# Two reorderings inside the eight slots of a chunked delta-rule scan: right sides ahead of the state updates on TensorE, and the matching swaps on VectorE and ScalarE

## The chip, the cores and the metric

The kernel runs on one NeuronCore of a Trainium2 chip. The metric is the device time of one execution in microseconds (us); the median over runs counts. TensorE is called PE below, with its weight loads (PEld) apart, VectorE is DVE, ScalarE is ACT, GpSimd is POOL, and SyncE (SP) issues all DMAs of the inner loop.

## The reference, cut to what matters

The input is 32 sequences of 512 tokens with 256 features: 8 heads of 32. A recurrent layer keeps for each head a 32x32 state S and takes two steps for each token: one that decays S, one that writes the pair (k, v). Both subtract what the state already answers to k:

```
bS = einsum('bhk,bhkv->bhv', b_t, S)
S  = exp(g)[..., None] * S + a_t[..., None] * bS[:, :, None, :] + k_t[..., None] * v_t[:, :, None, :]
o  = einsum('bhk,bhkv->bhv', q_t, S)
```

Here q, k, v are silu(x W), g and beta are projections too, and k is normalised. The outputs are gated, normalised for each head and projected by Wo. Then follow x + attention, a layer norm, one dense layer with a low-rank addition, and a second layer norm.

## The kernel before, in words

The work is cut into 32 groups of 512 tokens (32 sequences, 16 tokens each). Within a group the scan is solved by chunks: 16 steps of 8 tokens are made into a small triangular system, whose inverse (t_t) is worked out one group ahead, so that the scan itself is only small matmuls of 32x32 tiles, four heads side by side on the array. A group has 8 chunks, and the main loop has one **slot** for each: n = 0 to 7. PE does in a slot, in this order:

- `deltas()` (L707, 64 matmuls): inverse (t_now) times the turned right sides (x_now) of the slot before, into p2_bank.
- `updates()` (L695 and L699, 64 matmuls each, interleaved): the change of the state into ds_bank and the correction of the outputs into o_bank, from parts and delta, which ACT copied from p2_bank in the slot before.
- `right_sides()` (L716, 128 matmuls): the state s_now times keys and queries uq_now, into p1_bank.
- a piece of dense work for other groups, another for each slot: dense4 (L614), dense5 (L585: two sums for each of two inputs), dense6 (L667), dense7 (L678, transposes). Slots 0 and 1 hold besides two packages each of `scores()` (L687), which build the small system of the next group; the first of slot 0 waits for keys and queries staged by DMA (uq_a from uqv). L562 are the projections.

DVE does in a slot `update` (called by scan_part: it waits for p3_filled, the end of updates(); two halves of the outputs at L1063, then moved = state + ds_bank at L1069), `turn_right_sides` (called by turn_part: it waits for p1_filled, the end of right_sides(); subtracts the values at L1076 and transposes at L1079), and then its dense work. In slots 1 and 7 a piece of dense work stands between the two. In slot 7 that is the sum of x_row with the projected outputs (L1242), and after the turn DVE writes uqv for the next group but one (L1253, L1258), which SP then stages as uq_a (L346). In slot 5 the first dense work is L1194, which empties the banks that dense5 fills again. In slot 7 x_row's halves empty a bank that dense7 fills again.

ACT does in a slot `delta_part` (called by scan_part: waits for p3_filled and for DVE's o_added; three copies of p2_bank, L834 twice and L835) and `query_part` (waits for x_turned, DVE's transpose; one copy of the query part of p1_bank, L841), then its own dense work. POOL turns moved into the decayed state (L469).

SP has one queue, written out by hand. Its order in slot n is: t_now once deltas() is done; then, once updates() is done, aq_now (L388) and w_now (L390) for the next slot; then, once right_sides() is done and the state decayed, uq_now (L356) and s_now (L357) for the next slot:

```
sp.wait_ge(p3_filled.handle, left)
sp.dma_start(aq_now[:, :, :], ...)
sp.dma_start(by_pairs(w_now[:, :, :]), ...)
...
sp.wait_ge(state_ready.handle, kept)
sp.wait_ge(p1_filled.handle, left)
stage_first(c if n < CH - 1 else 1 - c, (n + 1) % CH)
```

The change leaves SP and POOL alone. "Block" below is the run of deltas, updates and right sides of one slot on PE.

Of the kernel before, what the change touches and what calls it, by code (L numbers as in the profile page):

```python
# [74 lines left out]
def delta_block(nc, x, xt, wq, wk, wv, wf1, wf2, wbeta, wog1, wog2, norm_w, wo, ffn_wt, ffn_b,  # L75
# [36 lines left out]
    with ExitStack() as ctx:  # L112
# [404 lines left out]
        def _(pe):  # L517
# [193 lines left out]
            def right_sides():  # L711

                for m in range(CT):
                    for b in range(GB):
                        for h in range(HPH):
                            mm = pe.matmul(p1_bank[quarter(h), m, b, :], s_now[quarter(h), m, b, :],  # L716
                                           uq_of(uq_now, m % HF)[quarter(h), m // HF, b * RQ:(b + 1) * RQ],
                                           start=True, stop=True)
                mm.then_inc(p1_filled.handle, 1)

            def slot(j, s):
# [8 lines left out]
                pe.wait_ge(set_up.handle, N_SET_UP)  # L730
                pe.wait_ge(w_in.handle, turn16)
# [93 lines left out]
        def _(act):  # L825
# [56 lines left out]
            def iteration(j, c):  # L882
# [10 lines left out]
                if there(j):  # L893
                    inverse_out(j)
                scan_part(0)
                query(0)
# [15 lines left out]

                scan_part(1)
                query(1)
# [17 lines left out]

                scan_part(2)
                query(2)
# [16 lines left out]

                scan_part(3)
                query(3)
# [24 lines left out]

                scan_part(4)
                query(4)  # L980
# [5 lines left out]

                scan_part(5)
                query(5)
# [20 lines left out]

                scan_part(6)  # L1010
                query(6)
# [5 lines left out]

                scan_part(7)
                query(7)
# [12 lines left out]
        def _(dve):  # L1032
# [91 lines left out]
            def iteration(j, c):  # L1124
# [9 lines left out]

                scan_part(0)
                turn_part(0)
# [13 lines left out]

                scan_part(1)
# [5 lines left out]
                turn_part(1)  # L1157
# [3 lines left out]

                scan_part(2)
                turn_part(2)
# [5 lines left out]

                scan_part(3)  # L1170
                turn_part(3)
# [4 lines left out]

                scan_part(4)
                turn_part(4)
# [8 lines left out]

                scan_part(5)
                turn_part(5)
# [27 lines left out]

                scan_part(6)
                turn_part(6)
# [16 lines left out]

                scan_part(7)
# [7 lines left out]
                turn_part(7)  # L1245
# [68 lines left out]
```

## Time and profile before

| what | value |
|---|---|
| median of 3 runs | 2699.11 us (2698.57 to 2700.31) |
| the profiled execution | 2707.01 us |
| its span, first to last instruction | 2705.2 us |
| mean granted TensorE clock in it | 0.940 |
| PE busy | 2298.0 us, 85% |
| ACT, DVE, POOL busy | 60%, 59%, 17% |
| DMA | 339.10 MB, mean 125 GB/s |

The span is that of the profiled execution; 1.8 us of its time lie outside it, and it is 7.9 us (0.3%) above the median. The granted clock is a share of TensorE's full 2.4 GHz: it has two levels here, 1.00 and 0.50, and in the stretch from 600 to 2350 us its mean is 0.98. In a matmul row the first number after the start is the time from the first start to the last end of all the matmuls of the row.

### The profile page before, as it was taken

How to read it: one execution, taken by the hardware profiler on the slowest of the kernel's cores; microseconds unless marked ns; L12 is line 12 of the kernel's file. 1: busy time of each engine (PE TensorE's matmuls, PEld its weight loads, DVE VectorE, ACT ScalarE, POOL GpSimd, SP SyncE). 2: the span in 40 equal slices, each digit the busy share in tenths (PEclk: the TensorE clock that was granted, in tenths of full speed). 3: DMA queues.
4: the chain of work that ended last, by engine and by line, in shares of the span. 5: the costliest groups of instructions: out<-in, count | busy, mean ns of one | idle time of the engine just before them, and what ended most of it. 6: DMA issues, size and time to landing. Idle time of an engine off the chain costs nothing.

```text
span 2705.2 us, 224996 instructions
## 1 busy us (share of the span) xinstructions
PE 2298.0 (85%) x102472; PEld 1742.0 (64%) x102472; DVE 1605.1 (59%) x3940; ACT 1629.6 (60%) x3048; POOL 459.2 (17%) x555
## 2 busy tenths in 40 slices
PE   4778878988888898888889888888988888888875
PEld 2466656666666666666667666666666666666664
DVE  2455356655666665566666556666655666665543
ACT  2555445666666666666666666666665666666544
POOL 1011111111111111111111111111211111121110
PEclk8789789999999999999999999999999999999887
DMA  3334443455555445555544555554445555444541
GB/s 76 84 102 109 112 124 102 123 141 141 146 131 139 117 123 136 142 144 140 138 118 123 133 138 142 144 136 121 122 134 137 140 144 134 130 120 121 134 121 49
DMA packets 692946, 339.10 MB, mean 125 GB/s; under 512 B 551794, under 2 KB 651728, under 8 KB 692816
## 3 DMA queue, kind: packets, MB, share of 16 engines
q1 hardware_dynamic: 692816, 337.67, 47.1%
q8 instruction: 44, 0.72, 0.1%
q14 instruction: 86, 0.70, 0.1%
HBM read 35.57 MB, written 16.78 MB: 19 GB/s over the span
## 4 chain that ended last, share of the span: by engine, by line
PE 77%; issue 10%; DVE 7%; DMA 4%; ACT 1%; SPq 0%; DVEq 0%; ACTq 0%
PE bank L562 14%; PE bank L716 10%; PE bank L695 9%; PE bank L687 9%; PE bank L707 6%; PE bank L585 4%; PE bank L699 4%; PE bank L667 4%; PE bank L614 4%; DMA uq_a<-uqv 4%; PE bank L569 2%; PE bank L629 2%; DVE uqv L1253 2%; PE bank L594 2%; PE bank L579 2%
## 5 line engine op out<-in xcount | busy, mean ns | idle before, releaser
L469 POOL TENSOR_TENSOR state<-moved,edge 128x512 f32<-128x512 f32 x252 | 292.6, 1161 | 1891.5 <-DVE moved L1069 1891.5
L834 ACT ACTIVATE parts<-bank,cf 128x256 f32<-128x256 f32 x512 | 215.1, 471 | 363.6 <-DVE o_col L1063 358.0
L695 PE MATMUL bank<-parts,w_now 32*32 32x64 f32 x16512 | 414.5, 221 | 5.7 <-DMA w_now<-w_row 2.9
L562 PE MATMUL bank<-x_col,w_kqv 128*128 128x512 f32 x768 | 376.3, 634 | 37.1 <-issue 36.4
L699 PE MATMUL bank<-aq_now,delta 32*32 32x16 f32 x16512 | 398.4, 178 | 5.2 <-issue 5.2
L699 PEld LDWEIGHTS bank<-aq_now,delta 32*32 32x32 f32 x16512 | 386.5, 109 | 2.1 <-issue 2.1
L695 PEld LDWEIGHTS bank<-parts,w_now 32*32 32x32 f32 x16512 | 373.4, 110 | 18.1 <-issue 5.9
L716 PE MATMUL bank<-uq_now,s_now 32*32 32x24 f32 x32768 | 360.3, 188 | 18.7 <-issue 18.6
L716 PEld LDWEIGHTS bank<-uq_now,s_now 32*32 32x32 f32 x32768 | 334.1, 106 | 29.5 <-issue 23.0
L1063 DVE TENSOR_TENSOR o_col<-qs,bank 128x64 f32<-128x64 f32 x512 | 89.7, 217 | 431.6 <-PE bank L699 427.8
L1092 DVE COPY_PREDICATED aq<-ci,bank 128x128 f32<-128x128 int32 x256 | 77.1, 301 | 434.2 <-PE bank L687 358.7
L562 PEld LDWEIGHTS bank<-x_col,w_kqv 128*128 128x128 f32 x768 | 148.9, 205 | 197.5 <-issue 192.3
L707 PEld LDWEIGHTS bank<-x_now,t_now 32*32 32x32 f32 x16448 | 168.4, 106 | 156.0 <-issue 154.2
L707 PE MATMUL bank<-x_now,t_now 32*32 32x32 f32 x16448 | 195.1, 195 | 69.5 <-issue 60.5
L687 PE MATMUL bank<-uq_a,w_a 32*32 32x48 f32 x8192 | 144.1, 242 | 115.9 <-DMA uq_a<-uqv 90.5
L687 PEld LDWEIGHTS bank<-uq_a,w_a 32*32 32x32 f32 x8192 | 134.4, 136 | 123.3 <-issue 107.4
L878 ACT ACTIVATE a_low<-bank 128x256 f32<-128x256 f32 x256 | 133.8, 624 | 112.1 <-PE bank L687 111.6
L841 ACT ACTIVATE qs<-bank 128x128 f32<-128x128 f32 x256 | 71.4, 279 | 204.3 <-DVE x_now L1079 202.3
L1121 DVE TENSOR_TENSOR inv<-inv,prod 128x60 f32<-128x60 f32 (+7 forms) x480 | 169.5, 353 | 16.5
L1117 DVE TENSOR_TENSOR prod<-low,inv 128x60 f32<-128x60 f32 (+7 forms) x480 | 165.9, 346 | 17.4 <-ACT low L949 4.1
L1069 DVE TENSOR_TENSOR moved<-state,bank 128x512 f32<-128x512 f32 x256 | 174.2, 680 | 0.0
L667 PE MATMUL bank<-w_out,y_col 128*128 128x256 f32 x512 | 121.2, 391 | 27.0 <-issue 23.6
(99 smaller groups left out, 3801.6 us busy)
## 6 DMA issues: line engine op xcount, KB each, us to landing
s_now<-state SPq DMA_DIRECT2D x256, 256.0 KB, 2.7
uq_now<-uqv SPq DMA_DIRECT2D x256, 192.0 KB, 2.6
t_now<-t_t SPq DMA_DIRECT2D x256, 128.0 KB
w_now<-w_row SPq DMA_DIRECT2D x256, 128.0 KB
uq_a<-uqv SPq DMA_DIRECT2D x64, 384.0 KB
low<-uqv SPq DMA_DIRECT2D x64, 384.0 KB
x_col<-in_xt_dram SPq DMA_DIRECT2D x32, 512.0 KB, 3.7
w_a<-w_col SPq DMA_DIRECT2D x64, 256.0 KB
```

The costliest lines, as they stand in the source:

```text
L469: pool.tensor_tensor(state[:, qc, :, :, :].rearrange("p m b v -> p (m b) v"), moved[m % 2][:, :, :, :].rearrange("p m b v -> p (m b) v"), ...
L562: mm = pe.matmul(ps[:, :], w_kqv[:, a, w, f * P:(f + 1) * P], x_col[:, a, :], start=a == 0, stop=a == KT - 1)
L667: mm = pe.matmul(ps[:, t * D:(t + 1) * D], y_col[:, f, own], w_out[:, f, :], start=f == 0, stop=f == HF - 1)
L687: mm = pe.matmul(a_banks[m // CT][quarter(h), m % CT, :, :].rearrange("p b r -> p (b r)"), w_a[c][quarter(h), m, :], uq_of(uq_a[c], m % HF ...
L695: pe.matmul(ds_bank[quarter(h), m, :, :].rearrange("p b v -> p (b v)"), w_now[quarter(h), m, :], parts[quarter(h), m, :, :].rearrange("p b ...
L699: mm = pe.matmul(o_bank[quarter(h), m, :], delta[quarter(h), m, :], aq_now[quarter(h), m, :], start=True, stop=True)
L707: mm = pe.matmul(p2_bank[quarter(h), m, :], t_now[quarter(h), m, :], x_now[quarter(h), m, :], start=True, stop=True)
L716: mm = pe.matmul(p1_bank[quarter(h), m, b, :], s_now[quarter(h), m, b, :], uq_of(uq_now, m % HF)[quarter(h), m // HF, b * RQ:(b + 1) * RQ] ...
L834: act.activation(parts[:, :, b, :], p2_bank, ACT.Copy, scale=cf[:, C_TAKE + b:C_TAKE + b + 1])
L1069: dve.tensor_tensor(moved[m % 2][:, :, :, :], mine, ds_bank, ALU.add).then_inc(s_added.handle, 1)
L1117: dve.tensor_tensor(step, low[:, p + 1:ROWS, :, p:p + 1].to_broadcast(size), inv[:, p:p + 1, :, 0:width].to_broadcast(size), ALU.mult).the ...
L1121: dve.tensor_tensor(inv[:, p + 1:ROWS, :, 0:width], inv[:, p + 1:ROWS, :, 0:width], step, ALU.add).then_inc(solve_step.handle, 1)
```

## The change

PE takes right_sides() in front of updates(); its waits move with it. DVE takes turn_part(n) in front of scan_part(n) in all slots; in slots 1 and 7 it thereby also passes the dense work that stood between the two. ACT takes query(n) in front of scan_part(n). No instruction is added or removed.

```diff
@@ PE, slot(j, s), after deltas() @@
                 pe.wait_ge(set_up.handle, N_SET_UP)
+                pe.wait_ge(uq_in.handle, turn16)
+                pe.wait_ge(s_in.handle, turn16)
+                pe.wait_ge(qs_copied.handle, turn)
+                right_sides()
+
+                pe.wait_ge(set_up.handle, N_SET_UP)
                 pe.wait_ge(w_in.handle, turn16)
                 pe.wait_ge(aq_in.handle, turn16)
                 pe.wait_ge(s_added.handle, turn)
                 updates()
-
-                pe.wait_ge(set_up.handle, N_SET_UP)
-                pe.wait_ge(uq_in.handle, turn16)
-                pe.wait_ge(s_in.handle, turn16)
-                pe.wait_ge(qs_copied.handle, turn)
-                right_sides()
@@ ACT, iteration(j, c), the same for all eight slots @@
+                query(1)
                 scan_part(1)
-                query(1)
@@ DVE, iteration(j, c), slots 0 and 2 to 6 @@
+                turn_part(2)
                 scan_part(2)
-                turn_part(2)
@@ DVE, slot 1 @@
+                turn_part(1)
                 scan_part(1)
                 if back:
                     ...
                     dve.scalar_tensor_tensor(y_col[:, :, :], gate[1 - c][:, :, :], 1.0, o_col[:, :, :], ALU.add,
                                              ALU.mult).then_inc(y_ready.handle, 1)
-                turn_part(1)
@@ DVE, slot 7 @@
+                turn_part(7)
                 scan_part(7)
                 if back:
                     dve.wait_ge(x_row_in.handle, x_row_in.at(j - 1, 16))
                     ...
                                           ALU.add).then_inc(drained["wo"].handle, 1)
-                turn_part(7)
                 if front:
```

## Rows read from the trace of the kernel before

**Rows 1.** The page's chain that ended last, shares of the span by engine.
```profile
PE 77%; issue 10%; DVE 7%; DMA 4%; ACT 1%; SPq 0%; DVEq 0%; ACTq 0%
```
**Rows 2.** Waits, whole span: us in total, times, longest.
```profile
PE bank L687 <- DMA uq_a<-uqv: 90.5, 27, 14.4
...
PE bank L707 <- DVE x_now L1079: 7.3, 5, 1.6
```
**Rows 3.** Timeline of PE, slot 7 and slot 0 of one group.
```profile
1324.11 0.25 PE L699 MATMUL bank<-aq_now,delta 32*32 32x16 f32 x8
1324.27 1.41 PE L716 MATMUL bank<-uq_now,s_now 32*32 32x24 f32 x128
...
1328.52 0.75 PE L707 MATMUL bank<-x_now,t_now 32*32 32x32 f32 x64
...
1334.90 2.78 PE L687 MATMUL bank<-uq_a,w_a 32*32 32x48 f32 x128 [2.87 <-DMA uq_a<-uqv]
```
**Rows 4.** Timeline of DVE, slot 7 of the same group.
```profile
1324.44 0.35 DVE L1063 TENSOR_TENSOR o_col<-qs,bank 128x64 f32<-128x64 f32 x2 [0.59 <-PE bank L699]
...
1325.30 1.28 DVE L1242 TENSOR_TENSOR x_row<-x_row,bank 128x512 f32<-128x512 f32 x2
1326.50 0.29 DVE L1076 TENSOR_TENSOR bank<-bank,uqv 128x128 f32<-128x128 f32 x1
...
1327.20 2.72 DVE L1253 TENSOR_TENSOR uqv<-kb_col,ep 128x512 f32<-128x512 f32 x4
```
**Rows 5.** The page's costliest groups: ACT's copies into parts.
```profile
L834 ACT ACTIVATE parts<-bank,cf 128x256 f32<-128x256 f32 x512 | 215.1, 471 | 363.6 <-DVE o_col L1063 358.0
```
**Rows 6.** Timeline of PE and of DVE, slot 5 of the same group.
```profile
1308.29 1.41 PE L716 MATMUL bank<-uq_now,s_now 32*32 32x24 f32 x128
1310.40 1.98 PE L585 MATMUL bank<-r_col,cf 128*128 128x512 f32 x4 [0.70 <-issue]
...
1314.03 0.75 PE L707 MATMUL bank<-x_now,t_now 32*32 32x32 f32 x64
...
1310.46 1.25 DVE L1194 TENSOR_TENSOR h_row<-h_row,bank 128x512 f32<-128x512 f32 x2
```
**Rows 7.** Timeline of SP's DMA issues in slots 7, 0 and 1.
```profile
1324.43 0.47 SPq L388 DMA_DIRECT2D aq_now<-aq  x1
...
1331.20 0.59 SPq L346 DMA_DIRECT2D uq_a<-uqv  x1
...
1349.15 0.62 SPq L390 DMA_DIRECT2D w_now<-w_row  x1
1350.03 0.62 SPq L356 DMA_DIRECT2D uq_now<-uqv  x1
1350.70 0.64 SPq L357 DMA_DIRECT2D s_now<-state  x1
```
**Rows 8.** Issue to landing of s_now: page (median, all), and slot 7 alone.
```profile
s_now<-state SPq DMA_DIRECT2D x256, 256.0 KB, 2.7
...
DMA to landing us min/median/max: 3.3/3.3/3.3
```
**Rows 9.** Windows: length, busy PE, PEld, DVE, ACT, POOL, granted clock, DMA share, GB/s.
```profile
1256.26:1256.38 0.12, 0.11 (x9) 0.12 (x13) 0.00 (x0) 0.12 (x1) 0.00 (x0) 1.00 0.91 221
...
2119.98:2120.30 0.32, 0.00 (x0) 0.00 (x0) 0.18 (x3) 0.10 (x1) 0.00 (x0) 0.50 0.90 220
...
249.50:252.80 3.30, 3.30 (x198) 3.30 (x191) 3.09 (x9) 1.43 (x2) 0.00 (x0) 0.50 0.47 155
...
1334.90:1338.20 3.30, 3.29 (x129) 3.10 (x130) 0.46 (x2) 0.89 (x4) 0.00 (x0) 0.50 0.90 218
```
**Rows 10.** Timeline of PE: a wait in the start-up, the first scores of two later groups.
```profile
249.07 0.89 PE L707 MATMUL bank<-x_now,t_now 32*32 32x32 f32 x64 [1.33 <-DVE x_now L1079]
...
2041.46 2.78 PE L687 MATMUL bank<-uq_a,w_a 32*32 32x48 f32 x128 [2.78 <-DMA uq_a<-uqv]
...
2120.37 2.78 PE L687 MATMUL bank<-uq_a,w_a 32*32 32x48 f32 x128 [3.10 <-DMA uq_a<-uqv]
```

More of the change, by code:

```diff
@@ L894, in iteration @@
                     inverse_out(j)
+                query(0)
                 scan_part(0)
-                query(0)
                 if there(j - 3):
@@ L931, in iteration @@
                     low_part(j + 1, 3)
+                query(2)
                 scan_part(2)
-                query(2)
                 if next_one:
@@ L950, in iteration @@
                                            scale=-1.0).then_inc(drained["nt"].handle, 1)
+                query(3)
                 scan_part(3)
-                query(3)
                 if back:
@@ L977, in iteration @@
                                        ACT.Exp, scale=-1.0).then_inc(drained["f"].handle, 1)
+                query(4)
                 scan_part(4)
-                query(4)
                 if front:
@@ L985, in iteration @@
                                    bias=one).then_inc(f_logged.handle, 1)
+                query(5)
                 scan_part(5)
-                query(5)
                 if back:
@@ L1008, in iteration @@
                         act.activation(both[half, :, :, b, :], inv[half, :, :, :], ACT.Copy).then_inc(inv_spread.handle, 1)
+                query(6)
                 scan_part(6)
-                query(6)
                 if front:
@@ L1016, in iteration @@
                     act.activation(ep[:, :, :, :], ep[:, :, :, :], ACT.Exp, scale=-1.0).then_inc(ep_ready.handle, 1)
+                query(7)
                 scan_part(7)
-                query(7)
             for j in range(-2, FIRST):
@@ L1133, in turn_part @@
                         turn_right_sides(j, c, n)
+                turn_part(0)
                 scan_part(0)
-                turn_part(0)
                 if there(j - 3):
@@ L1168, in iteration @@
                     last.then_inc(w_turned.handle, 1)
+                turn_part(3)
                 scan_part(3)
-                turn_part(3)
                 if next_one:
@@ L1175, in iteration @@
                     solve(j + 1, 0, 8)
+                turn_part(4)
                 scan_part(4)
-                turn_part(4)
                 if next_one:
@@ L1186, in iteration @@
                     solve(j + 1, 11, ROWS - 1)
+                turn_part(5)
                 scan_part(5)
-                turn_part(5)
                 if out_of:
```

2 lines of the change are left out of this document (1 added, 1 removed).

## The prediction

> **What bounds the kernel now.** I read the page's chain first. PE holds 77% of it and its own issue gaps 10% [rows 1]: in most slots PE simply works from its block into its dense piece into the next block, and nothing that DVE or ACT does can be felt. The list of waits says the same from the other side. What the change makes earlier is the turned right sides, and in the whole span PE waited 7.3 us for those, five times [rows 2]. The one wait of PE that recurs is 90.5 us, 27 times, for the DMA of uq_a, in front of the first scores() of slot 0 [rows 2].
>
> Then the timelines, for what feeds that wait. PE's updates of slot 7 end at 1324.36 and its right sides at 1325.68; the deltas of slot 0 start at 1328.52, its block ends at 1332.03, and the scores start at 1334.90 after 2.87 us of idle [rows 3]. DVE starts its update at 1324.44, 0.08 after PE's last update matmul, having waited for it. It follows with x_row at 1325.30, the turn at 1326.50 and uqv at 1327.20 [rows 4]. SP issues uq_a at 1331.20 [rows 7], which lets the scores go 3.70 later. So once a group the path is: end of updates in slot 7, DVE's four jobs, DMA, scores. All else is PE.
>
> Last the windows, for the clock. Behind that idle, from 1334.90 to 1338.20, the granted clock is 0.50, that is 1.2 GHz [rows 9]. PE worked through all of that stretch, so it cost half of 3.30, 1.65 us.
>
> **Part 1, slot 7: the chain starts later.** Right sides take 1325.68 - 1324.36 = 1.32 us of PE. With them in front, the updates end where the block ends, at 1325.68, so DVE's update starts at 1325.76 instead of 1324.44. Its length up to x_row is 0.86 (1324.44 to 1325.30), x_row's is 1.20 (to 1326.50), both [rows 4], so uqv would start at 1327.82. The turn, 0.70 us (1326.50 to 1327.20), leaves this chain: right sides now end at about 1324.1, the turn fits before 1325.1, and DVE would idle until 1325.76. Against 1327.20 the chain is 1.32 - 0.70 = **0.62 us later**. If DVE came late to slot 7 the loss would be less; it waited 0.59 for PE there [rows 4], so it does not. With the 27 waits of [rows 2] that is 17 us.
>
> **Part 2, slot 5.** DVE's L1194 starts 1310.46 - 1309.70 = 0.76 after the block's end [rows 6]; with turn first and update last it starts 0.08 + 0.86 = 0.94 after it. It must empty a bank before the second pair of L585 matmuls. These are due at 0.70 + 0.99 = 1.69 after the block, and half of L1194 is done at 0.94 + 0.63 = 1.57 [rows 6], to which a signal's delay comes. Below: nothing. Above: 0.2 us in each of 32 groups, 6 us. I take 0.1, 3 us.
>
> **Part 3, SP's queue, which is not reordered.** uq_now and s_now stand behind the wait for updates(), and their own wait for right_sides() is now long over. So they gain nothing from right sides being early, while their user, the next right_sides(), comes earlier. From the block's end: aq_now is issued at 0.07 (1324.43 against 1324.36 [rows 3, 7]), w_now at 0.6; it takes 0.62, and uq_now follows 0.88 after it where nothing is waited for (1349.15 to 1350.03); s_now 0.67 later [rows 7]. That is an issue at 2.1 to 2.2. With 2.7 to landing it is there at 4.9, with 3.3, as in slot 7, at 5.5 [rows 8]. The user: from the block of slot 5 to the next deltas are 1314.03 - 1309.70 = 4.33 us, and 0.7 for deltas makes 5.0 [rows 6]. Slots 4 to 6 have such a short dense piece, and the margin is 0.1. I take 0, by the median landing; at the long landing it would be 0.4 in three slots of some 27 groups, 32 us. Behind these waits on SP stand only t_now and the next group's staging, which are wanted later. In slot 0 the case is plain: deltas are done at 2.84 + 0.7 = 3.5 after slot 7's block [rows 3], s_now lands at 4.9 to 5.5, so PE stands 1.4 to 2.0 there. That is covered: the block of slot 0 ends at 1333.4 to 1334.0, the scores could not start before 1334.90 + 0.62 = 1335.5. Without that cover it would cost 1.4 to 2.0 a group.
>
> **Part 4, the rest.** DVE's update and ACT's copies now fall wholly behind the block, and the next deltas wait for them: 0.08 + 0.3 for the outputs, then two copies of 0.47 [rows 5] and one more like them, done at about 1.9. The shortest way to the next deltas is 2.84 us (slot 7) [rows 3]. So they cost nothing, with 0.9 to spare. ACT's query copy is out of the way earlier; no one waited for it. In slot 1, DVE's turn also passes the gate product: nothing, as the next deltas are a whole package of scores away. POOL's decay starts 1.3 later in each slot, and is wanted a slot later.
>
> **Part 5, the clock.** The sum so far is +17 + 3 = +20 us. But the idle of 2.87 in front of the scores is what goes before the low clock, and the change breaks it up: 1.4 to 2.0 between deltas and right sides, and 1.5 to 2.1 in front of the scores. If the clock then stays up, each of some 25 groups wins 1.65 and loses 0.7, 24 us in all. What speaks for a half-way answer: much of the span runs on a rhythm. From 1334.90 to 2041.46 [rows 3, 10] are nine groups of 78.51 us in the mean, though the next alone took 78.91 (to 2120.37). The level changes don't follow the matmuls: at 1256.26 to 1256.38 scores already ran and the clock was still 1.00, and at 2119.98 to 2120.30, in front of late scores, it was already 0.50 [rows 9]. A late group thus spends part of its low stretch in idle and catches up. By the same gate, a group with the change is 78.5 + 0.7 = 79.2 where the low level hits and 77.6 where it doesn't, and each moves the next one's idle, one way or the other, against the gate's own rhythm. I expect a mixture of both sorts that keeps near 78.5: low in about (78.5 - 77.6) / 1.65 = 55% of the groups. That takes 0.45 x 1.65 x 25 = 19 us back from 20, and leaves +1; for the first and last groups, which don't keep this rhythm, I add 2. Against the profiled execution (2707.0) that is 2710, against the median of the runs **2702 us**.
>
> The Trainium skill, in TensorE: Matmul & The Clock Gate, What's actually happening, has the gate watch activity on a period that does not restart with the program; the rows at 1256 and 2120 agree.
>
> **The rivals.** *A, the low clock stays in every group.* Any idle of this size is enough: in the start-up PE waited only 1.33 us up to 249.07 [rows 10], and the clock was at 0.50 from 249.50 on [rows 9]. Against it: that is a single case, outside the rhythm of the main loop. Then the sum stands: 2699 + 20 = 2719, and up to 2722 with slot 5 at its upper bound. *B, the clock never falls.* The longest idle is now 2.1 instead of 2.9. Then 2699 + 20 - 1.65 x 25 = 2678. This is the other side: faster, and it decides from the point where the gate misses more than 60% of the groups. The Trainium skill, TensorE: Matmul & The Clock Gate, Why this matters for your kernels, warns of one long gap between bursts of matmuls and has nothing against two shorter ones: read strictly, that is this rival. *C, s_now is late in slots 5 to 7 too.* 0.4 a slot, or 1.2 a group, on top of 0.7: 80.4 with the low clock, 78.8 without, no longer balanced by it: 2699 + 20 + 32 = 2751 at worst, and some 2715 to 2725 if the wait is 0.1 to 0.3 and the clock gives some of it back. For it speaks the margin of only 0.1; against it that landings have a median of 2.7 and the 3.3 was in the one slot where other DMAs crowd behind. *D, the turn's earliness is worth something by itself.* Only the 7.3 us of [rows 2] could be won, and they lie in the start-up; with the rest as forecast it would be 2695. I give it nothing apart from the others.
>
> **How the numbers follow.** The measurement can't tell less than 0.2%, 5.4 us, from no change. The balanced case has 0.45 and its own range is 2696 to 2708, from the ends of part 2 and one low stretch more or less at either end; a tenth of it lies above 2704.5. A has 0.20 (2715 to 2722), C 0.15 (2710 to 2751), B 0.20 (2678 to 2693, for a gate that misses nearly all or most). Slower 0.20 + 0.15 + 0.05 = 0.40, within 0.2% 0.40, faster 0.20. The range is 2682 to 2724: it leaves out the upper half of C and the lower end of B.
>
> **What would show it.** In the profile after: uqv's L1253 starting 2.1 after the end of slot 7's block instead of 1.5; DVE's turn inside an idle in front of the update; s_now issued 2.1 to 2.2 after the block and a PE wait for it in front of L716 in slot 0, with none in slots 5 to 7; a wait for uq_a of 1.5 to 2.1 left; first scores at 2.78 in some groups and 1.56 in others, and starts of these 78.5 apart in the mean. If all of them are 2.78, it is A; if none, B; if L716 waits for s_now in slots 5 to 7, C. I am wrong altogether if some wait appears that I have covered, above all ACT's copies in front of deltas in slot 0.

## The result, and the profile after

The changed kernel takes **2751.02 us** (median of 4 runs, 2743.53 to 2754.8) against 2699.71 for the kernel before on the same chip: a ratio of 1.0182, interval 1.0154 to 1.021. It is slower by 51 us, where 2702 was forecast and 2724 was the upper end. Its profiled execution took 2753.76 us for a span of 2752.0, 46.8 more than before's.

The page of the changed kernel: the chain that ended last, the busy times of the engines, and the group of right-sides matmuls.
```profile
PE 77%; issue 8%; DVE 7%; DMA 6%; SPq 1%; ACT 1%; DVEq 0%; POOL 0%; ACTq 0%
...
PE 2329.8 (85%) x102472; PEld 1755.9 (64%) x102472; DVE 1674.0 (61%) x3940; ACT 1631.5 (59%) x3048; POOL 528.0 (19%) x555
...
L716 PE MATMUL bank<-uq_now,s_now 32*32 32x24 f32 x32768 | 367.4, 191 | 76.3 <-DMA s_now<-state 69.6
```
DMA has 6% of the chain instead of 4% [rows 1]. The third row says which DMA: s_now, in front of right sides. The lists of waits of the changed kernel, first over the whole span, then for 0 to 540 us, for 600 to 2350 and for 2350 to the end (us in total, times, longest):
```profile
PE bank L716 <- DMA s_now<-state: 69.6, 44, 2.7
PE bank L687 <- DMA uq_a<-uqv: 54.3, 27, 14.4
...
PE bank L716 <- DMA s_now<-state: 13.7, 9, 2.7
...
PE bank L716 <- DMA s_now<-state: 33.6, 22, 1.8
...
PE bank L716 <- DMA s_now<-state: 20.8, 12, 2.4
```
The wait for uq_a has shrunk from 90.5 to 54.3 us [rows 2]. The new wait has two parts. In the main loop it comes 22 times in 22 groups, once in each, 33.6 us or 1.53 in the mean; it is the one forecast for slot 0. But it comes 21 times more at the two ends, 34.5 us, in few groups. (One more, of some 1.5 us, lies between these windows.)

Where the span grew is seen from the starts of the first deltas (L707) of a slot 0, here from the timeline of PE, before and after, at the sixth group and 24 groups later. Of the kernel before:
```profile
543.32 0.75 PE L707 MATMUL bank<-x_now,t_now 32*32 32x32 f32 x64
...
2427.70 0.83 PE L707 MATMUL bank<-x_now,t_now 32*32 32x32 f32 x64
```
Of the changed kernel:
```profile
553.01 0.75 PE L707 MATMUL bank<-x_now,t_now 32*32 32x32 f32 x64
...
2454.05 0.75 PE L707 MATMUL bank<-x_now,t_now 32*32 32x32 f32 x64
```
So the start grew by 9.7 us, the 24 groups between by 1901.0 - 1884.4 = 16.6 (79.21 a group instead of 78.52), and the end, 2752.0 - 2454.1 = 297.9 instead of 277.5, by 20.4. **Two thirds of the loss lie outside the main loop**, in this one profiled execution of each kernel; the runs of the changed kernel spread over 11 us.

Inside it, the same starts give the length of each slot, from its deltas to the next slot's (us, means; "warm" are the 8 of 24 groups whose work never met the low clock; the kernel before has no such group, and its warm row is an estimate from the six of experiment e2_before_warm, less the 0.47 that its added branch costs in slot 1):

| slot | 0 | 1 | 2 | 3 | 4 | 5 | 6 | 7 | group |
|---|---|---|---|---|---|---|---|---|---|
| before, mean | 15.26 | 11.59 | 9.56 | 11.68 | 7.94 | 8.00 | 8.03 | 6.46 | 78.52 |
| before, warm | 14.03 | 11.61 | 9.54 | 11.64 | 7.92 | 7.98 | 8.03 | 6.45 | 77.2 |
| after, mean | 14.38 | 11.61 | 9.54 | 11.69 | 8.97 | 8.19 | 8.03 | 6.80 | 79.21 |
| after, warm | 14.35 | 11.60 | 9.55 | 11.64 | 7.93 | 8.20 | 8.02 | 6.80 | 78.1 |

By the rows "warm", the change adds 0.9 us of waiting to a group: 0.3 in slot 0, 0.2 in slot 5, 0.35 in slot 7. By "mean" less "warm" the low clock costs 1.3 before and 1.1 after. It gave back 0.2, 5 us in all.

**Slots 7 and 0 of one group of the changed kernel**: the timeline of PE, then of DVE, of SP's DMA issues and of POOL.
```profile
1266.73 0.25 PE L699 MATMUL bank<-aq_now,delta 32*32 32x16 f32 x8
1267.87 2.32 PE L678 MATMUL bank<-cf,both 128*128 128x128 f32 x16 [0.89 <-issue]
1270.12 0.75 PE L707 MATMUL bank<-x_now,t_now 32*32 32x32 f32 x64
1272.22 1.26 PE L716 MATMUL bank<-uq_now,s_now 32*32 32x24 f32 x128 [1.35 <-DMA s_now<-state]
...
1277.03 1.57 PE L687 MATMUL bank<-uq_a,w_a 32*32 32x48 f32 x128 [1.94 <-DMA uq_a<-uqv]
```
```profile
1265.81 0.45 DVE L1079 STREAM_TRANSPOSE x_now<-bank 128x256 f32<-128x256 f32 x1
1267.06 0.35 DVE L1063 TENSOR_TENSOR o_col<-qs,bank 128x64 f32<-128x64 f32 x2 [0.80 <-PE bank L699]
...
1267.92 1.28 DVE L1243 TENSOR_TENSOR x_row<-x_row,bank 128x512 f32<-128x512 f32 x2
1269.12 2.78 DVE L1253 TENSOR_TENSOR uqv<-kb_col,ep 128x512 f32<-128x512 f32 x4
1271.82 1.46 DVE L1258 TENSOR_TENSOR uqv<-q_col,ep 128x512 f32<-128x512 f32 x2
```
```profile
1269.14 0.64 SPq L357 DMA_DIRECT2D s_now<-state  x1
...
1273.37 0.59 SPq L346 DMA_DIRECT2D uq_a<-uqv  x1
```
```profile
1269.22 1.46 POOL L496 TENSOR_TENSOR edge<-ep,em 128x32 f32<-128x32 f32 x2
1270.63 1.40 POOL L501 TENSOR_TENSOR edge<-tail,em 128x32 f32<-128x32 f32 x2
```
The block of slot 7 ends with the updates at 1266.98. DVE has turned (until 1266.26) and waits 0.80 for it, and uqv begins 2.14 behind it, where 2.1 was forecast. s_now is issued 2.16 behind it (forecast 2.1 to 2.2), and right sides wait 1.35 for it. The first scores take 1.57 instead of 2.78 [rows 3]: the clock is up. From the end of the block to the scores are 10.05 us, where they were 9.22 [rows 3]: 0.83 more, not 0.62, and DVE's and SP's rows say where. From the start of uqv to the issue of uq_a are 4.25 us instead of 4.00 [rows 4, 7].

**What became of the low clock.** Windows of the changed kernel (length, busy PE, PEld, DVE, ACT, POOL, granted clock, DMA share, GB/s) in one group's slots 3 and 4, and at the first scores of the next:
```profile
992.50:995.80 3.30, 3.30 (x15) 1.68 (x13) 3.06 (x8) 2.69 (x5) 0.00 (x0) 1.00 0.00 0
996.00:999.20 3.20, 3.20 (x213) 3.03 (x216) 0.18 (x2) 2.19 (x3) 2.78 (x4) 0.50 0.13 44
1002.80:1006.00 3.20, 3.20 (x9) 2.52 (x8) 3.03 (x7) 1.33 (x3) 1.02 (x1) 0.50 0.74 202
1037.34:1038.90 1.56, 1.56 (x128) 1.44 (x128) 1.56 (x6) 1.11 (x3) 0.57 (x1) 1.00 0.94 235
```
and slot 4 in the timeline of PE, in a warm group and then in this one:
```profile
917.85 0.75 PE L707 MATMUL bank<-x_now,t_now 32*32 32x32 f32 x64
918.56 1.40 PE L716 MATMUL bank<-uq_now,s_now 32*32 32x24 f32 x128
922.14 3.72 PE L614 MATMUL bank<-w_ffn,a_low 128*128 128x256 f32 x16 [0.58 <-issue]
...
996.17 1.08 PE L707 MATMUL bank<-x_now,t_now 32*32 32x32 f32 x64
997.08 1.92 PE L716 MATMUL bank<-uq_now,s_now 32*32 32x24 f32 x128
1001.84 5.80 PE L614 MATMUL bank<-w_ffn,a_low 128*128 128x256 f32 x16 [0.27 <-issue]
```
The low stretch has left the first scores, where it was in every group before, and reaches slot 4 in 14 of the 24 groups: for 3.4 us in nine of them, of about 79 us, and for 10.2 us in one piece, three times as long, in five, of 81.6 to 81.7 us, of which this is one. (Six groups also have 3.4 us of it in slot 0, ahead of the scores, where it costs 0.3 at most.) In this group the deltas of slot 4 take 1.08 instead of 0.75 and its dense piece 5.80 instead of 3.72. No idle stands just ahead of it: in the 3.30 us before, PE was busy for 3.30, and the only gap in its work since 980 us is one of 0.61, at 988.7.

**The last groups.** PE's timeline there:
```profile
2641.61 1.08 PE L707 MATMUL bank<-x_now,t_now 32*32 32x32 f32 x64 [1.87 <-ACT delta L835]
2644.70 1.92 PE L716 MATMUL bank<-uq_now,s_now 32*32 32x24 f32 x128 [2.01 <-DMA s_now<-state]
...
2651.06 1.08 PE L707 MATMUL bank<-x_now,t_now 32*32 32x32 f32 x64 [1.87 <-ACT delta L835]
```
These slots have no dense piece. PE stands 1.87 us for ACT's copies, which are now behind the block, and another 2.0 for s_now, which SP issues after aq_now and w_now. One slot is 9.45 us long. The same part of the kernel before:
```profile
2607.94 1.03 PE L707 MATMUL bank<-x_now,t_now 32*32 32x32 f32 x64 [1.64 <-DVE x_now L1079]
...
2614.14 0.74 PE L707 MATMUL bank<-x_now,t_now 32*32 32x32 f32 x64 [1.36 <-DVE x_now L1079]
```
There a slot was 6.20 us: deltas waited 1.36 to 1.64 for the turned right sides, and nothing waited for s_now. The rest of the difference goes with the clock, which was granted at 0.50 in that slot and at 0.72 in this one. Over the whole last part PE is busy for 212.3 us instead of 207.0, with the same instructions and a granted clock of 0.81 instead of 0.84: of the 20.4 us, 5.3 are slower work and the rest is standing.

### The profile page after: what moved, and what is told of

Its sections match the earlier page's. It is cut to its first block, busy times and chain, and to the rows that moved or that the text cites. A ratio compares the mean times of both kernels' runs of the same rounds, so it can differ in the third digit from the quotient of the medians.

```text
span 2752.0 us, 225191 instructions
## 1 busy us (share of the span) xinstructions
PE 2329.8 (85%) x102472; PEld 1755.9 (64%) x102472; DVE 1674.0 (61%) x3940; ACT 1631.5 (59%) x3048; POOL 528.0 (19%) x555
## 4 chain that ended last, share of the span: by engine, by line
PE 77%; issue 8%; DVE 7%; DMA 6%; SPq 1%; ACT 1%; DVEq 0%; POOL 0%; ACTq 0%
PE bank L562 13%; PE bank L716 12%; PE bank L695 10%; PE bank L687 8%; PE bank L707 6%; PE bank L614 5%; PE bank L699 5%; PE bank L667 4%; PE bank L585 4%; DMA uq_a<-uqv 3%; DVE uqv L1253 2%; PE bank L569 2%; PE bank L629 2%; PE bank L594 2%; DMA s_now<-state 2%
## 5 line engine op out<-in xcount | busy, mean ns | idle before, releaser
L469 POOL TENSOR_TENSOR state<-moved,edge 128x512 f32<-128x512 f32 x252 | 324.2, 1286 | 1882.3 <-DVE moved L1069 1882.3
L695 PE MATMUL bank<-parts,w_now 32*32 32x64 f32 x16512 | 438.3, 228 | 12.8 <-issue 9.3
L699 PE MATMUL bank<-aq_now,delta 32*32 32x16 f32 x16512 | 420.1, 182 | 7.9 <-issue 7.9
L699 PEld LDWEIGHTS bank<-aq_now,delta 32*32 32x32 f32 x16512 | 409.4, 114 | 8.3 <-issue 8.3
L695 PEld LDWEIGHTS bank<-parts,w_now 32*32 32x32 f32 x16512 | 385.7, 113 | 27.8 <-issue 16.4
L716 PEld LDWEIGHTS bank<-uq_now,s_now 32*32 32x32 f32 x32768 | 344.1, 110 | 90.5 <-issue 77.3
L562 PE MATMUL bank<-x_col,w_kqv 128*128 128x512 f32 x768 | 364.5, 618 | 33.0 <-issue 32.1
L1076 DVE TENSOR_TENSOR bank<-bank,uqv 128x128 f32<-128x128 f32 x256 | 76.2, 298 | 362.6 <-PE bank L716 362.5
L707 PEld LDWEIGHTS bank<-x_now,t_now 32*32 32x32 f32 x16448 | 173.5, 109 | 157.8 <-issue 157.8
L707 PE MATMUL bank<-x_now,t_now 32*32 32x32 f32 x16448 | 200.6, 198 | 71.3 <-issue 59.5
L1121 DVE TENSOR_TENSOR inv<-inv,prod 128x60 f32<-128x60 f32 (+7 forms) x480 | 215.3, 448 | 16.5
L1117 DVE TENSOR_TENSOR prod<-low,inv 128x60 f32<-128x60 f32 (+7 forms) x480 | 167.8, 350 | 17.4 <-ACT low L949 4.1
L687 PE MATMUL bank<-uq_a,w_a 32*32 32x48 f32 x8192 | 113.6, 212 | 74.9 <-DMA uq_a<-uqv 54.3
L687 PEld LDWEIGHTS bank<-uq_a,w_a 32*32 32x32 f32 x8192 | 105.3, 113 | 81.5 <-issue 65.6
```

Of the source, the lines that this page charges most:

```text
L469: pool.tensor_tensor(state[:, qc, :, :, :].rearrange("p m b v -> p (m b) v"), moved[m % 2][:, :, :, :].rearrange("p m b v -> p (m b) v"), ...
L562: mm = pe.matmul(ps[:, :], w_kqv[:, a, w, f * P:(f + 1) * P], x_col[:, a, :], start=a == 0, stop=a == KT - 1)
L687: mm = pe.matmul(a_banks[m // CT][quarter(h), m % CT, :, :].rearrange("p b r -> p (b r)"), w_a[c][quarter(h), m, :], uq_of(uq_a[c], m % HF ...
L695: pe.matmul(ds_bank[quarter(h), m, :, :].rearrange("p b v -> p (b v)"), w_now[quarter(h), m, :], parts[quarter(h), m, :, :].rearrange("p b ...
L699: mm = pe.matmul(o_bank[quarter(h), m, :], delta[quarter(h), m, :], aq_now[quarter(h), m, :], start=True, stop=True)
L707: mm = pe.matmul(p2_bank[quarter(h), m, :], t_now[quarter(h), m, :], x_now[quarter(h), m, :], start=True, stop=True)
```

## The experiments

Where a kernel has "fillers", it multiplies by the identity into a bank that is overwritten later: work that is added, with no use. "First" is up to the sixth group's slot 0, "group" the mean of the 24 that follow, "last" the rest of the span; these three are from one profiled execution each. A ratio is to the kernel before as timed on the same chip, where its median was 2698.0 to 2703.3; the experiments ran on four chips, so they are compared by ratio and not by median.

| kernel | median us | ratio to before, interval | first | group | last |
|---|---|---|---|---|---|
| before | 2699.71 | | 543.3 | 78.52 | 277.5 |
| changed | 2751.02 | 1.0182, 1.0154 to 1.021 | 553.0 | 79.21 | 297.9 |
| e1_sp_order | 2769.62 | 1.0259, 1.0241 to 1.0277 | 537.0 | 80.93 | 280.5 |
| e2_before_warm | 2699.01 | 0.9989, 0.9976 to 1.0002 | 538.4 | 78.50 | 277.7 |
| e3_pe_order_alone | 2814.56 | 1.0411, 1.0384 to 1.0437 | 558.0 | 81.35 | 304.0 |
| e4_xrow_first | 2753.53 | 1.0189, 1.0164 to 1.0215 | 552.1 | 79.35 | 298.5 |
| e5_before_two_fillers | 2711.27 | 1.0015, 0.999 to 1.004 | 541.2 | 78.56 | 284.2 |
| e6_after_two_fillers | 2790.81 | 1.0324, 1.0286 to 1.0362 | 557.2 | 80.36 | 309.0 |
| e7_sp_order_xrow_fillers | 2735.71 | 1.0131, 1.0091 to 1.0172 | 544.0 | 79.23 | 283.6 |
| e8_before_xrow_fillers | 2707.0 | 1.0022, 1.0005 to 1.0039 | 535.0 | 78.63 | 286.0 |
| e9_engines_order_alone | 2799.23 | 1.0373, 1.0338 to 1.0407 | 554.5 | 81.78 | 284.7 |
| e10_after_edges_later | 2746.66 | 1.018, 1.0148 to 1.0213 | 542.8 | 79.23 | 303.0 |
| e11_e7_edges_later | 2719.34 | 1.0084, 1.0059 to 1.0109 | 539.1 | 78.84 | 289.7 |
| e12_before_xrow_edges_f1 | 2697.46 | 0.9995, 0.9978 to 1.0013 | 533.7 | 78.53 | 282.0 |
| e13_sp_order_at_ends | 2719.64 | 1.0052, 1.0032 to 1.0072 | 538.3 | 79.34 | 280.9 |
| e14_e13_and_slot3_filler | 2731.46 | 1.0103, 1.0066 to 1.0139 | 541.2 | 79.35 | 283.8 |

Of the theories expected below, those of e10, e11 and e13 met their ranges. In e2, e4, e7, e8 and e12 the time was the rival's. e1, e3, e6, e9 and e14 came out slower than their theory allowed, and e5 slower than both.

**e1_sp_order.** The changed kernel, with SP's queue put in the order of PE's work:
```diff
@@ SP, in every slot @@
-                    if (there(j) or (there(j - 1) and n < 1)) and ...:
-                        ... aq_now, w_now
                     if there(j) and not (isinstance(j, int) and j == G - 1 and n == CH - 1):
                         ... uq_now, s_now
+                    if (there(j) or (there(j - 1) and n < 1)) and ...:
+                        ... aq_now, w_now
```


> The changed kernel, with SP's queue put in PE's new order: uq_now and s_now are issued as soon as right sides are done, before the wait for the updates. Theory (s_now is late because SP still waits for the updates): PE's 69.6 us of waits for s_now fall under 10 us; the last two groups, which have no long dense work to cover them, give back some 15 us, the first ones some 5. In the main loop slot 0 loses its stall, but PE then stands in one piece of about 3.7 us in front of the scores and the clock falls there again, so nothing or a loss of up to 10 us there. In all 2725 to 2740. Rival (the loss is in DVE's and ACT's later updates): 2751 within 5 us, the same tail as in the changed kernel.

All waits for s_now are gone, and the two ends win 16.0 and 17.4 us. But the main loop loses 41, where up to 10 was expected. Its groups are of 81.4 to 81.9 us for the most part, with the clock low for 5.8 in slot 0 and 2.4 in slot 4. PE's timeline, and two windows at and behind the scores:
```profile
1271.21 2.78 PE L687 MATMUL bank<-uq_a,w_a 32*32 32x48 f32 x128 [3.37 <-DMA uq_a<-uqv]
```
```profile
1269.90:1273.10 3.20, 1.89 (x96) 1.92 (x100) 0.95 (x7) 0.50 (x2) 0.22 (x1) 0.50 0.96 232
1273.30:1276.50 3.20, 3.20 (x39) 1.67 (x31) 1.95 (x7) 2.46 (x6) 0.00 (x0) 0.50 0.95 250
```
What follows: the late s_now splits the idle of slot 0 into 1.35 and 1.94, and this split is what keeps the first scores warm. As one idle of 3.37 it brings the low clock back, for longer than before. This part of the forecast (breaking the idle up is worth something) holds.

**e2_before_warm.** The kernel before, with PE kept at work in the idle of slot 0:
```diff
@@ PE, in front of the scores of slot 0 @@
-                        pe.wait_ge(a_staged[c].handle, staged)
                         ...
+                            with pe.If_lt(part, 1):
+                                for i in range(2):
+                                    pe.matmul(psum[3][:, :], ident, w_kqv[:, 0, 0:2, :]..., start=True, stop=True)
+                        pe.wait_ge(a_staged[c].handle, staged)
                         scores(c)
```


> The kernel before, with two extra matmuls of 512 columns (1.9 us, their result is overwritten by the scores) in PE's idle in front of the first scores of slot 0, so that it is never idle for long. Theory (a low clock of 3.4 us behind that idle costs 1.65 us in each group, and the rhythm of 78.5 us comes from it): first scores take 1.56 instead of 2.78, groups take about 76.9, 2699 - 25 x 1.6 = 2659. Rival (the 78.5 us have another bound, such as DVE's own chain around the group): 2695 to 2700 with the scores at 1.56 and the idle moved elsewhere.

The scores are warm, and the time is the same. Timeline of PE, and the window behind the deltas of slot 4, which start at 1291.66:
```profile
1250.95 1.59 PE L687 MATMUL bank<-uq_a,w_a 32*32 32x48 f32 x128 [0.47 <-DMA uq_a<-uqv]
```
```profile
1292.40:1295.60 3.20, 3.20 (x178) 3.20 (x181) 0.40 (x3) 1.43 (x4) 1.14 (x2) 0.50 0.12 41
```
In 18 of 24 groups the low stretch has moved to slot 4 (9.14 us there instead of 7.94), and the mean group is 78.50, to 0.02 what it was. Six groups had no low stretch: 77.67. So the low clock can be pushed out of the wait for uq_a, but it comes elsewhere. My Part 5 had taken for granted that a group that escapes it in slot 0 escapes it altogether.

**e3_pe_order_alone** and **e9_engines_order_alone.** The change has two parts, and each was run alone. e3 is the kernel before with only PE's order changed; e9 the changed kernel with PE's old order (each with the waits that belong to it):
```diff
@@ e3: before, PE in every slot @@
+                right_sides()
                 updates()
-                right_sides()
@@ e9: after, PE in every slot @@
-                right_sides()
                 updates()
+                right_sides()
```


> One part alone: PE takes right sides first, DVE and ACT keep the order of before (updates, then the turn; copies, then the query). Theory (the chain of slot 7 is what PE's order makes late, and the turn's place in front takes 0.7 back): DVE's turn is back between x_row and uqv, so uqv starts 1.3 later than before instead of 0.6; some 0.7 a group worse than the changed kernel, 2760 to 2775. Rival (DVE's and ACT's new order is the harm): 2700 to 2735.

> The other part alone: PE keeps updates in front of right sides, DVE and ACT take the new order (turn before update, query before the copies). DVE's turn then waits for the block's end and the update stands behind it, so slot 7's uqv starts 0.1 + 0.7 + 0.9 + 1.2 = 2.9 after the block instead of 1.5, 1.3 to 1.4 later than before. Theory (the chain of slot 7 and nothing else of this counts): no late s_now, so the last two groups stay at 278 us; main loop groups some 1.4 longer than clean ones of before, 78.6 or, where the clock falls, 80 to 82: 2720 to 2770. Rival (new order on DVE and ACT is good by itself): 2700 or less.

Both are far worse than the two together: 2815 and 2799 against 2751. In e3 the four warm groups are of 79.28 (slot 0 14.83, slot 5 8.85), since DVE turns last what PE now makes first, and uqv in slot 7 and L1194 in slot 5 come behind that; the other 20 have 6.8 us of low clock. In e9 DVE's turn waits for right sides that PE makes last, and the update and the first dense work of DVE stand behind the turn. So PE waits for the banks that these empty: 14.6 us in slot 5 (for L1194) and 15.8 in slot 7 (for x_row) in the main loop, and without a low stretch these slots take 8.85 and 7.41 us. Slot 4 is 8.86 in the mean by the clock alone (7.93 where it is up). 22 of 24 groups have a low stretch. The order of PE and that of the other two engines are worth nothing apart. Together each takes back part of the other's loss.

**e4_xrow_first.** Slot 7's dense piece (L678) takes 2.32 us in the changed kernel where it took 1.96. Its bank is emptied by x_row, which is behind the update:
```diff
@@ DVE, slot 7 of the changed kernel @@
                 turn_part(7)
-                scan_part(7)
                 if back:
                     ... x_row
+                scan_part(7)
```


> The changed kernel, with DVE's sum of x_row in slot 7 in front of the update instead of behind it, in the idle that it has there. Theory (slot 7's chain is 0.6 to 0.9 too long): uqv starts about 0.8 earlier than in the changed kernel, and dense7 no longer waits for a bank; 0.8 x 25 = 20 us less, 2731, unless the clock takes some of it by falling in other places (2725 to 2745). Rival (the chain does not set the group's length, the clock in slot 4 does): within 5 us of 2751.

Slot 7 falls from 6.80 to 6.42, so the wait is what I took it for. The time is unchanged: right sides of slot 0 now wait 42.2 us for s_now in the main loop instead of 33.6. And the chain to the scores is no shorter. DVE's and POOL's timelines in slot 7:
```profile
1261.01 3.55 DVE L1253 TENSOR_TENSOR uqv<-kb_col,ep 128x512 f32<-128x512 f32 x4
```
```profile
1261.17 1.43 POOL L469 TENSOR_TENSOR state<-moved,edge 128x512 f32<-128x512 f32 x1 [6.56 <-DVE moved L1069]
```
The block ends at 1259.56, so uqv starts 1.45 behind it instead of 2.14, 0.7 earlier where 0.8 was expected. But its first four products now fall beside POOL's decay and take 3.55 us instead of 2.78, and uq_a is issued at 1265.99, 4.98 after their start instead of 4.25. The scores start 10.08 behind the block, where it was 10.05.

**e5 to e8: fillers in two places.** In slot 0 as in e2, and one in slot 3, behind expand_both(), ahead of the slot 4 that the low clock moved to:
```diff
@@ PE, slot 3 @@
                     expand_both(j)
+                    if there(j + 1):
+                        pe.wait_ge(drained["nt"].handle, drained["nt"].at(j + 1, 4 * GB))
+                        pe.matmul(psum[3][:, 0:D], ident, w_kqv[:, 0, 0, :], start=True, stop=True)
```
e5 is the kernel before with them, e6 the changed one, e7 the changed one with e1's and e4's edits too, e8 the kernel before with e4's edit.

> The kernel before with filler matmuls in two places: two of 512 columns in slot 0's idle, and one of 256 columns (0.5 us) at the end of slot 3's dense work, in front of which the low clock went when slot 0 alone was filled. Theory (groups are held at 78.5 us by the clock, which falls in one place if not in the other): no low clock in the main loop, slot 4 at 7.9 in every group, groups of 77.4 to 77.9 plus 0.5, so 78.1, no longer held at 78.5: 2685 to 2695. Rival (something else holds 78.5): 2699 as with one filler.

> The changed kernel with the same two fillers. Theory (the change costs 1.1 to 1.2 us a group by waits, and the rest of its loss in the main loop is the clock in slot 4): no low clock in the main loop, the groups of 81.7 are gone, all are 78.1 + 0.9 = 79.0 or a little less, and it stays 35 to 50 us over the kernel before with the same fillers, of which some 17 lie in the last groups. Rival (groups of 81.7 come from a wait, not from the clock): they are still there, and the time is 2760 or more.

> The changed kernel with SP's queue in PE's new order, x_row first on DVE in slot 7, and both fillers. Theory: it takes away all three costs found so far, the waits for s_now, the longer chain of slot 7, and the clock: groups of 78.1 to 78.4, the last groups as short as before: 2688 to 2702, level with the kernel before. Rival (PE's order itself is worse in the main loop, whatever is moved around it): 2720 or more, with groups over 79.

> The kernel before with x_row in front of the update on DVE in slot 7, and both fillers. Theory (slot 7's chain through DVE sets when the scores start): uqv starts 0.5 to 0.6 earlier than before and the group is as much shorter, 77.5: 2672 to 2685, the fastest. Rival (PE in slot 0 is bound by its fillers and block, so nothing is left to win): as the kernel before with two fillers.

In e5, 18 of 24 groups are warm, at 78.23, and the mean is 78.56: the fillers' own cost (0.47 in slot 1 for the branch, 0.65 in slot 3) stands for the low clock's. e6 has its filler of slot 0 behind the late s_now and overruns (warm groups 79.57, slot 0 14.8). e7 has 19 warm groups at 79.01, its ends are within 7 us of those of before, and it is still 1.3% slower. Its uqv write takes 3.55 us beside POOL's work where it took 2.72 [rows 4]:
```profile
1334.88 3.55 DVE L1262 TENSOR_TENSOR uqv<-kb_col,ep 128x512 f32<-128x512 f32 x4
```

**e10 to e12: POOL out of DVE's way.** POOL's small edge products (L496, L501) fall beside DVE's uqv products in slot 7. They are made to wait:
```diff
@@ POOL, slot 7 @@
                     pool.wait_ge(em_ready.handle, em_ready.at(g, 1))
+                    pool.wait_ge(q_ready.handle, q_ready.at(g, 1))
```
e10 is the changed kernel with it, e11 is e7 with it, e12 is e8 with it and one filler in slot 0 instead of two.

> The changed kernel, with POOL's four small edge products of slot 7 held back until DVE has written uqv. Theory (DVE and POOL slow each other when they work at the same time, and in the changed kernel POOL's edges fall on L1258): L1258 back from 0.76 to 0.68 us each, the edges back from 0.7 to 0.3 each, uq_a issued 0.2 earlier; clean groups 77.9 instead of 78.1, in all 0 to 10 us less, within the spread of the changed kernel (2743 to 2755). Rival (their times grow for another reason): the same durations as in the changed kernel.

> The kernel with SP's order, x_row first and both fillers, and POOL's edges held back in the same way. There L1253's four took 3.55 us instead of 2.7, beside POOL. Theory: L1253 falls to at most 3.0 (POOL's decay alone is left beside it), L1258 to 1.3, uq_a goes 0.5 to 0.8 earlier, groups without low clock 79.0 to 78.4: 2715 to 2725 against 2736. Rival (not POOL): L1253 still 3.5 and 2736.

> The kernel before with x_row first on DVE in slot 7, POOL's edges held back, one filler of 512 columns in slot 0 and one of 256 at the end of slot 3. Theory: uqv goes 0.5 earlier than before without being stretched by POOL, slot 0 is no longer bound by its filler, groups without low clock 77.7: 2680 to 2695, faster than the kernel before. Rival (the clock takes it all back in another place, or slot 0 is bound by PE): 2700.

The groups of the tiles, min/median/max ns of one, in the changed kernel:
```profile
L496 POOL TENSOR_TENSOR edge<-ep,em x64: 310/756/764, 44.9 to 2539.1; 128x32 f32<-128x32 f32 x64
...
L1258 DVE TENSOR_TENSOR uqv<-q_col,ep x64: 677/756/783, 50.1 to 2541.6; 128x512 f32<-128x512 f32 x64
```
and in e10:
```profile
L497 POOL TENSOR_TENSOR edge<-ep,em x64: 298/302/307, 51.2 to 2532.0; 128x32 f32<-128x32 f32 x64
...
L1259 DVE TENSOR_TENSOR uqv<-q_col,ep x64: 676/681/685, 49.7 to 2530.9; 128x512 f32<-128x512 f32 x64
```
So the two slow each other, and apart each takes about its shortest time in the changed kernel. Slot 0 gets 0.3 to 0.5 us shorter by it in e10. Yet the mean group stays at 79.23, since the clock is now low in slot 4 in 22 of 24 groups, for 4.4 us in the mean. In e11, where fillers keep most groups warm, the 0.35 arrives (79.01 to 78.66 in warm groups). e12 has the shortest warm group of the kernels with both fillers, 77.99, and still a mean of 78.53: the kernel before, not beaten (0.9995, 0.9978 to 1.0013).

**e13_sp_order_at_ends.** Since e1 wins at the ends and loses in the middle, the changed kernel was run with SP's new order only where the slots are written out one by one, outside the loop:
```diff
@@ SP, in every slot; j is an int only outside the main loop @@
+                    if isinstance(j, int):
+                        for_right_sides()
+                        for_updates()
+                    else:
+                        for_updates()
+                        for_right_sides()
```


> The changed kernel with SP's new order only in the groups outside the main loop (the first five and the last five iterations), the changed kernel's own order inside it. Theory (some 30 of the 50 us are waits for s_now in groups whose slots are short or start cold, and the main loop costs 17 for reasons of its own): up to the sixth group 537 to 543 instead of 553, the part from the thirtieth group on 281 instead of 298, the main loop unchanged at 79.2 a group: 2715 to 2730. Rival (SP's order at the ends matters only together with the main loop's): 2740 or more.

Its ratio is 1.0052 where the changed kernel's was 1.0182, 35 us less. Both ends together take 819.2 us, where the changed kernel took 850.9 and the one before 820.8. The waits of e13 at its two ends, 0 to 540 and from 2350 on, and PE's timeline in the last groups:
```profile
PE bank L725 <- DMA s_now<-state: 1.3, 1, 1.3
...
PE bank L725 <- DMA s_now<-state: 3.1, 3, 1.3
```
```profile
2624.89 0.74 PE L716 MATMUL bank<-x_now,t_now 32*32 32x32 f32 x64 [1.90 <-ACT delta L844]
2626.03 1.92 PE L725 MATMUL bank<-uq_now,s_now 32*32 32x24 f32 x128 [0.39 <-DMA s_now<-state]
```
Of 34.5 us of waits 30 are gone, and so are 31.7 us of span. **The loss at the ends, taken together, is that of the late s_now**, with the low clock that goes along with it. For the last part this is plain in every kernel: 297.9 to 309.0 us in the five with the late s_now (changed, e3, e4, e6, e10), 280.5 to 289.7 in the six without it there (e1, e7, e9, e11, e13, e14), whatever else they change. For the first part it isn't: e10 has 14.4 us of the same waits there and takes 542.8, as the kernel before does, and e9 has none and takes 554.5. So how the 30 us divide between the two ends is open. The wait for ACT's copies is still there, 1.9, but it stands about where the wait for the turn stood before.

**e14_e13_and_slot3_filler.** e13 with the filler of slot 3 alone, to tell whether slot 4's low clock can be had back without touching slot 0.

> The same, with the filler of 256 columns at the end of slot 3's dense work and none in slot 0. Theory (the groups of 81.7 are the low clock staying for two stretches in slot 4): slot 4 at 7.9 and no group of 81 or more; groups of 78.1 + 0.6 = 78.7, or up to 79.1 where the clock is low in slot 0's block; main loop 78.7 to 79.1: 2705 to 2725, level with or under the kernel without the filler. Rival (the long groups have another cause): they stay, and the filler's 0.6 x 24 = 15 us come on top.

Slot 4 falls to 8.09 and 18 groups are warm, at 78.75. The other six are of 81.2, with 3.4 low in slot 0 again and 3.4 around slots 3 and 4. The mean is 79.35, as in e13, though the low clock fell from 5.0 us a group to 1.7: the filler itself costs 0.65 in slot 3, and where the low clock now falls in slot 0 it hits the projections behind the scores. PE's timeline:
```profile
785.84 5.29 PE L571 MATMUL bank<-x_col,w_kqv 128*128 128x512 f32 x8
```
They take 3.69 in a warm group. By the medians e14 is the slower of the two, by 12 us.

## Why the prediction was wrong

**The step that failed: Part 3, and the claim that the s_now wait is "covered".** Its numbers for the main loop were right: issue 2.16 behind the block, 1.35 of wait in slot 0 (1.53 in the mean; 1.4 to 2.0 forecast), none in slots 5 to 7. I priced it there, where the wait for uq_a comes next and hides it, and took the ends as "+2". But at the start and in the last groups there are slots with little or no dense work. There s_now is late 21 times, and each time PE stands bare, for 1.6 us in the mean and up to 2.7. The ends cost 9.7 + 20.4 = 30 of the 47 us instead of 2, and e13, with SP's queue in the new order there, has them back at the length of before (819.2 against 820.8). A last part that much longer stands in every kernel with the late s_now (20 to 32 us over before); the 9.7 of the first part could be had back without touching it (e10), so their cause is not settled. Part 3 itself held the warning, that without cover it would cost 1.4 to 2.0. I didn't ask in which groups the cover is absent.

**Part 5, the clock, failed too: it gave back 5 us, not 19.** Waits broken up do keep the first scores warm, in all groups and not just 45% of them. But the low stretch moved to slot 4 in 14 of 24 groups, and in five of these it stays three times as long. A mean group is 79.21, not 78.5. Nor is 1.65 us its price wherever it falls. A stretch of 3.4 us cost 1.2 at the scores (slot 0 of e2 against before), 0.9 in slot 4 of the changed kernel (8.80 against 7.93), 0.3 at most ahead of the scores, and 1.6 at the projections (5.29 against 3.69, e14). With e2 and e12 it is shown that taking away the idle in front of one low stretch moves it and need not remove it. Why slot 4, and why sometimes three times as long, stays open: PE was busy ahead of it.

The forecast balance at 78.5 does turn up, but in the kernels with the old order: before, e2, e5, e8 and e12 all lie at 78.50 to 78.63, though their warm groups run from 77.2 to 78.2. The changed kernel, e4, e10, e13 and e14, all with the new order on the three engines and SP's old one in the loop, lie at 79.21 to 79.35, with warm groups, where they have any, of 77.9 to 78.75. (e6, whose filler overruns, lies apart at 80.36.) So within each order the mean did not follow the warm group. That is what these runs have in common, not a law that they prove, and what sets the two values is open.

**Part 1 was right in its mechanism and a little small in size.** uqv starts 2.14 behind the block, as forecast, but then DVE and POOL meet, for 0.25 more (e10, e11 show it): the chain is 0.83 longer, not 0.62. I had named the four jobs of DVE but not who waits for the second: slot 7's own dense piece waits for x_row's bank, 0.35. That is no cost beside the chain, for it passes while the chain runs anyway: in e4 it is gone from slot 7 and stands in slot 0. By the table slots 7 and 0 together are 0.67 longer in a warm group; what takes 0.83 down to this isn't shown, and the warm row of before is an estimate.

**Part 2**: slot 5 is longer by 0.2, the upper end that I gave, 0.1 more than taken. **Part 4**: in the main loop ACT's copies cost nothing, as said, and slots 1 to 4 and 6 keep their warm length. Only in the last groups do deltas wait 1.87 for them, instead of 1.36 to 1.64 for the turn; the forecast had the copies done at about 1.9. POOL's decay, 1.3 later, does meet DVE's solve in slot 3 (below), and this is hidden.

**The rivals.** C was 2751 at worst, and 2751.02 was measured, but by luck: its place was slots 5 to 7 of the main loop, and there is no such wait there. Its mechanism is right and its place wrong. A (low in every group's scores) didn't come: 1.57 in the scores. By the sign that the prediction gave for it, no scores at 2.78, B came; but B was that the clock never falls, and it fell elsewhere in 16 of 24 groups. D is void.

As a sum over the span, with the forecast in brackets: ends +30 (+2), waits in the main loop 24 x 0.9 = +21 (+20), clock 24 x -0.2 = -5 (-19): +46 (+3), against 46.8 measured. The waits of the main loop came out nearly as forecast; the ends and the clock did not.

## What to carry to other kernels

When one engine's order of work is changed, walk each of its inputs back through the queue that brings it. Here PE took right sides first and SP still fetched the updates' operands first. Price such a lateness in the start-up and in the last groups too: what covers it in the steady loop (dense work, a later wait) is missing there, and a few thin groups outweighed 24 thick ones. Where a loop has a stretch at the low clock, don't book its removal as a gain before the profile shows where that stretch went: here a filler in slot 0, a filler in slot 3 and a shorter chain each moved it, and none beat the kernel before. And when a job is moved to start earlier, look at what it then runs beside: in e4 uqv started 0.7 earlier beside POOL's decay and was done no sooner.

## What the runs showed of the hardware

**DVE and POOL slow each other.** In slot 3 of the changed kernel POOL's decay, later by the length of right sides, runs into DVE's first product of solve(). The timelines of POOL and of DVE:
```profile
1310.44 1.05 POOL L469 TENSOR_TENSOR state<-moved,edge 128x512 f32<-128x512 f32 x1 [8.48 <-DVE moved L1069]
```
```profile
1310.56 1.04 DVE L1121 TENSOR_TENSOR inv<-inv,prod 128x60 f32<-128x60 f32 x1
```
The same product took 0.27 us at most in the kernel before. Now it ends at 1311.60, 0.11 after POOL's. Busy time of POOL grew from 459.2 to 528.0 us over the span, DVE's from 1605.1 to 1674.0, with the same instructions. The Trainium skill, SBUF — State Buffer, the section "SBUF: two separate sides", says that a VectorE operation with two inputs in SBUF and a GpSimd one share a port pair that one holds for its whole instruction. The row of slot 3 agrees: DVE's product, begun 0.12 after POOL's, ends just behind it, and POOL's is not stretched (1.05). The uqv products beside the edges do not quite: an edge goes from 0.31 to 0.76, about one DVE product, but that product only from 0.68 to 0.76, less than an edge's length.

**The granted clock fell with no idle just ahead of it** (992.5 to 995.8: PE busy throughout, then 0.50), and its low time and the time of the kernel need not go together: one added matmul of 256 columns a group took the low clock from 5.0 to 1.7 us a group (e13 to e14), and the mean group stayed at 79.3 to 79.4.

**A low stretch costs by what it falls on.** Deltas of 32x32 took 1.08 us instead of 0.75 and right sides 1.92 instead of 1.40 (slot 4 of the changed kernel), 1.4 times as long and not twice; the scores took 2.78 instead of 1.57.
